# Rotary products of the queries moved from GpSimd to VectorE, with a padded hidden layer and another form of floor

## What is computed

```python
qkv = x @ Wqkv
q, k, v = jnp.split(qkv, 3, -1)
q = l2norm(q) * qs
k = l2norm(k) * ksc
q = q * cos * scale + rotate_half(q) * sin * scale
k = k * cos * inv + rotate_half(k) * sin * inv
out = local_attention(q, k, v)
return out @ Wo
```

## Time and profile before

| | us |
|---|---|
| median of 3 runs | 3893.35 |
| lowest and highest of them | 3887.17, 3898.36 |
| profiled execution, whole | 3903.03 |
| its span, first to last instruction | 3901.3 |
| transformer stage, first to last mask product, about | 1778 |

### The profile page before, as it was taken

How to read it: one execution, slowest core, us unless ns; L and a number is a source line. 1 busy time by engine, 2 the same in 40 slices (tenths; PEclk the granted TensorE clock), 3 DMA queues, 4 the chain that set the end, 5 groups by cost and what they waited for, 6 DMA issues and landing times. The chain is left out here.

```text
span 3901.3 us, 124853 instructions
## 1 busy us (share of the span) xinstructions
PE 3535.7 (91%) x52653; PEld 2416.1 (62%) x52653; DVE 2444.6 (63%) x5150; ACT 2288.7 (59%) x4664; POOL 2084.5 (53%) x2227
## 2 busy tenths in 40 slices
PE   7996999998999988999999999999999996968885
PEld 4664555544566655766676666676676775846664
DVE  4446445512566646777777777677677775568885
ACT  2233555522455555766776676676676775457775
POOL 2003000000121128888888888888888884177773
PEclk9997999999899999999999999999999997989997
DMA  1000000010000003112112211211211111121010
GB/s 27 2 3 24 1 1 1 1 31 7 1 2 2 2 18 85 48 49 70 47 48 60 58 48 46 73 47 45 72 48 46 47 48 25 31 79 24 21 24 20
DMA packets 155562, 130.09 MB, mean 33 GB/s; under 512 B 53592, under 2 KB 144768, under 8 KB 154112
## 3 DMA queue, kind: packets, MB, share of 16 engines
q1 hardware_dynamic: 155008, 122.09, 12.0%
HBM read 31.93 MB, written 3.54 MB: 9 GB/s over the span
## 5 line engine op out<-in xcount | busy, mean ns | idle before, releaser
L1055 PE MATMUL t_wa<-t_w_qkv,t_resid 128*128 128x512 f32 x1152 | 606.6, 627 | 16.2 <-DMA t_scales<-in_L_ffn_k_scale 11.8
L999 POOL TENSOR_TENSOR t_ra<-t_qn,t_rot 128x512 f32<-128x512 f32 x384 | 490.1, 1276 | 179.3 <-DVE t_qn L1310 175.4
L1205 ACT ACTIVATE t_sq<-t_wa 128x512 f32<-128x512 f32 x384 | 227.6, 593 | 172.8 <-PE t_wa L1055 171.7
L3037 DVE TENSOR_REDUCE a_nmax<-a_A 128x2 f32<-128x1024 f32 (+3 forms) x256 | 206.1, 823 | 126.9 <-PE a_A L2935 124.6
L1345 DVE TENSOR_REDUCE t_nmax<-t_S 128x8 f32<-128x512 f32 x192 | 132.8, 692 | 238.1 <-PE t_S L1077 232.7
L1000 POOL TENSOR_TENSOR t_rb<-t_qn,t_rot 128x256 f32<-128x256 f32 x384 | 279.8, 729 | 0.0
L1001 POOL TENSOR_TENSOR t_rb<-t_qn,t_rot 128x256 f32<-128x256 f32 x384 | 279.6, 728 | 0.0
L3030 POOL TENSOR_SCALAR_AFFINE_SELECT a_pt<-a_pt 128x512 f32<-128x512 f32 x128 | 79.7, 634 | 371.9 <-ACT a_pt L3010 371.9
L1299 DVE TENSOR_REDUCE t_ssq<-t_sq 128x8 f32<-128x512 f32 x384 | 261.1, 683 | 17.9 <-ACT t_sq L1205 12.7
L1310 DVE SCALAR_TENSOR_TENSOR t_qn<-t_inv,t_wa 128x512 f32<-128x512 f32 x384 | 249.7, 680 | 13.0 <-POOL t_rb L1001 5.7
L1055 PEld LDWEIGHTS t_wa<-t_w_qkv,t_resid 128*128 128x128 f32 x1152 | 186.7, 195 | 113.9 <-issue 88.2
(11 more groups left out here) (498 smaller groups left out, 9340.0 us busy)
## 6 DMA issues: line engine op xcount, KB each, us to landing
t_vw<-t_vn SPq DMA_DIRECT2D x768, 66.0 KB
t_vw<-t_vn SPq DMA_DIRECT2D x672, 33.0 KB
t_w_qkv<-in_L_ffn_Wqkv SPq DMA_DIRECT2D x6, 1536.0 KB, 6.6
t_v<-t_vn SPq DMA_DIRECT2D x56, 132.0 KB, 2.8
t_vw<-t_nothing SPq DMA_DIRECT2D x96, 33.0 KB
t_w_o<-in_L_ffn_Wo SPq DMA_DIRECT2D x6, 512.0 KB
f_h<-t_L_ffn_h_w SPq DMA_DIRECT2D x2, 1024.0 KB, 7.5
t_w<-in_L_ffn_W SPq DMA_DIRECT2D x6, 341.0 KB
```

The lines of the kernel that those rows point to most:

```text
L999: pool.tensor_tensor(ra[:, n % 2, r], qn[:, r], spread(cos, 1, 8), ALU.mult).then_inc(done.sem, 1)
L1055: pe.matmul(bank, resid[:, b, lo:lo + P], w_qkv[:, l % 2, at:at + 512], start=True, stop=True).then_inc(wa_up.sem, 1)
L1205: act.activation(sq[:, r].rearrange("p h d -> p (h d)"), wa[:, wa_job[kind, n] % 3, :], ACT.Square).then_inc(squared.sem, 1)
L3037: v.tensor_reduce(nmax[:, u % 2, t, :].rearrange("p (j e) -> p j e", e=32)[:, 2 * pair:2 * pair + 2, 0], A[:, 2 * pair:2 * pair + 2, 0:(t ...
```

## The change

- The queries are no longer normalised before the rotation. VectorE multiplies them with cosine and sine straight from the PSUM bank (`rotate_queries`, three instructions for each group, issued between `add_ffn` and the sum of the keys' squares). GpSimd adds the two parts and then, once `inv` is there, scales the sum by it, which commutes with the rotation. The keys keep their path, with `kn` in place of `qn[:, 1]`.
- The bank of the queries is claimed when ScalarE's squares and VectorE's three products of the group before are done.
- The floor is a reduction by maximum over pairs: `ssq` gets a second column that holds 1e-24, the sums are written to the first, and the result goes to `floor_ssq`.
- The third piece of the hidden layer is padded from 85 to 128 columns or rows in `w_1`, `w_2` and `b_1`. GpSimd fills the padding with zeros at the start, and SyncE's first load waits for all seven fills (before, the loads went first and the wait for four fills came behind).
- The banks are named by a table `WA` in place of the job number modulo 3. The order of the projections is left as it is.

```diff
+    WA = {"q": 0, "k": 1, "v": 2}
...
-        w_1 = st.sb("w_1", [P, 2, 2 * hid])
+        w_1 = st.sb("w_1", [P, 2, 2, NH * P])
...
-        ssq = st.sb("ssq", [P, 2, 16])
+        ssq = st.sb("ssq", [P, 2, 16, 2])
+        floor_ssq = st.sb("floor_ssq", [P, 2, 16])
...
-        qn = st.sb("qn", [P, 2, 8, HD])
+        kn = st.sb("kn", [P, 8, HD])
...
-                    sp.dma_start(w_1[:, z, :], w1[l]).then_inc(sem, 16)
+                    sp.dma_start(w_1[:, z, :, 0:hid], w1[l].rearrange("p (h n) -> p h n", h=2)).then_inc(sem, 16)
...
+                sp.wait_ge(zeroed, 7)
                 load(0)
-                sp.wait_ge(zeroed, 4)
...
+                pool.memset(w_1[:, :, :, hid:NH * P], 0.0).then_inc(zeroed, 1)
+                pool.memset(w_2[:, :, NH - 1, :], 0.0).then_inc(zeroed, 1)
+                pool.memset(b_1[:, :, :, NH - 1], 0.0).then_inc(zeroed, 1)
...
-                def rotate(kind, n):
-                    r, done = (0, q_rot) if kind == "q" else (1, k_rot)
+                def rotate_keys(n):
                     t = tile_of(n)
-                    cos, sin = rot[:, layer_of(t) % 2, 2 * r, t % TPB, :], rot[:, layer_of(t) % 2, 2 * r + 1, t % TPB, :]
-                    pool.wait_ge(normed.sem, normed.at(n, r + 1))
+                    cos, sin = rot[:, layer_of(t) % 2, 2, t % TPB, :], rot[:, layer_of(t) % 2, 3, t % TPB, :]
+                    if n % SLOTS == 0:
+                        pool.wait_ge(tables.sem, tables.at(layer_of(t), 6))
+                    pool.wait_ge(normed.sem, normed.at(n))
                     if n >= 2:
-                        pool.wait_ge(T_up.sem, T_up.at(T_job[kind, n - 2]))
-                    pool.tensor_tensor(ra[:, n % 2, r], qn[:, r], spread(cos, 1, 8), ALU.mult).then_inc(done.sem, 1)
-                    pool.tensor_tensor(rb[:, n % 2, r, :, 0:32], qn[:, r, :, 32:64], spread(sin[:, 0:32], 1, 8), ALU.mult).then_inc(done.sem, 1)
-                    pool.tensor_tensor(rb[:, n % 2, r, :, 32:64], qn[:, r, :, 0:32], spread(sin[:, 32:64], 1, 8), ALU.mult).then_inc(done.sem, 1)
+                        pool.wait_ge(T_up.sem, T_up.at(T_job["k", n - 2]))
+                    pool.tensor_tensor(ra[:, n % 2, 1], kn[:, :], spread(cos, 1, 8), ALU.mult).then_inc(k_rot.sem, 1)
+                    pool.tensor_tensor(rb[:, n % 2, 1, :, 0:32], kn[:, :, 32:64], spread(sin[:, 0:32], 1, 8), ALU.mult).then_inc(k_rot.sem, 1)
+                    pool.tensor_tensor(rb[:, n % 2, 1, :, 32:64], kn[:, :, 0:32], spread(sin[:, 32:64], 1, 8), ALU.mult).then_inc(k_rot.sem, 1)
 
                 for even, now, turn, mid, ahead, tail, ffn, last in slots():
                     if ffn is not None:
                         pool.wait_ge(lnd.sem, lnd.at(ffn, 3))
                         pool.tensor_tensor(rstd[:, :], vare[:, :], g["half"][:, 0:1], ALU.pow).then_inc(rooted.sem, 1)
                     if mid is not None:
-                        rotate("k", mid)
+                        rotate_keys(mid)
                         pool.wait_ge(k_rot.sem, k_rot.at(mid, 3))
                         pool.tensor_tensor(ra[:, mid % 2, 1], ra[:, mid % 2, 1], rb[:, mid % 2, 1], ALU.add).then_inc(k_roped.sem, 1)
                     if ahead is not None:
-                        if ahead % SLOTS == 0:
-                            pool.wait_ge(tables.sem, tables.at(layer_of(tile_of(ahead)), 6))
-                        rotate("q", ahead)
                         pool.wait_ge(q_rot.sem, q_rot.at(ahead, 3))
-                        pool.tensor_tensor(ra[:, ahead % 2, 0], ra[:, ahead % 2, 0], rb[:, ahead % 2, 0], ALU.add).then_inc(q_roped.sem, 1)
+                        pool.tensor_tensor(ra[:, ahead % 2, 0], ra[:, ahead % 2, 0], rb[:, ahead % 2, 0], ALU.add).then_inc(q_added.sem, 1)
+                        pool.wait_ge(q_added.sem, q_added.at(ahead))
+                        pool.wait_ge(inved.sem, inved.at(ahead))
+                        pool.tensor_tensor(ra[:, ahead % 2, 0], ra[:, ahead % 2, 0], spread(inv[:, ahead % 2, 0:8], 2, HD), ALU.mult).then_inc(q_roped.sem, 1)
...
+                        elif kind == "k":
+                            pe.wait_ge(normed.sem, normed.at(n - 1))
                         else:
-                            pe.wait_ge(normed.sem, normed.at(n - 1, 1 if kind == "q" else 2))
-                    return wa[:, wa_job[kind, n] % 3, :]
+                            pe.wait_ge(squared.sem, squared.at(n - 1, 1))
+                            pe.wait_ge(q_rot.sem, q_rot.at(n - 1, 3))
+                    return wa[:, WA[kind], :]
...
-                        for c, (at, size) in enumerate(HC):
-                            lo = half * hid + at
-                            m = pe.matmul(bank[0:size, c * P:(c + 1) * P], w_1[:, l % 2, lo:lo + size], lnT[:, :], start=True, stop=True)
+                        for c in range(NH):
+                            m = pe.matmul(bank[:, c * P:(c + 1) * P], w_1[:, l % 2, half, c * P:(c + 1) * P], lnT[:, :], start=True, stop=True)
...
+                v.memset(ssq[:, :, :, 1], 1e-24).then_inc(limits, 1)
+                v.wait_ge(limits, 1)
...
-                    v.tensor_reduce(ssq[:, n % 2, 8 * r:8 * r + 8], sq[:, r], X, ALU.add).then_inc(summed.sem, 1)
+                    v.tensor_reduce(ssq[:, n % 2, 8 * r:8 * r + 8, 0], sq[:, r], X, ALU.add).then_inc(summed.sem, 1)
 
                 def floor(n):
                     v.wait_ge(summed.sem, summed.at(n, 2))
-                    v.tensor_scalar(ssq[:, n % 2, :], ssq[:, n % 2, :], 1e-24, None, ALU.max).then_inc(floored.sem, 1)
-
-                def normalise(kind, n):
-                    r, read = (0, q_rot) if kind == "q" else (1, k_rot)
+                    v.tensor_reduce(floor_ssq[:, n % 2, :], ssq[:, n % 2, :, :], X, ALU.max).then_inc(floored.sem, 1)
+
+                def rotate_queries(n):
+                    t = tile_of(n)
+                    cos, sin = rot[:, layer_of(t) % 2, 0, t % TPB, :], rot[:, layer_of(t) % 2, 1, t % TPB, :]
+                    raw = wa[:, WA["q"], :].rearrange("p (h d) -> p h d", h=8)
+                    v.wait_ge(wa_up.sem, wa_up.at(wa_job["q", n]))
+                    if n % SLOTS == 0:
+                        v.wait_ge(tables.sem, tables.at(layer_of(t), 6))
+                    if n >= 2:
+                        v.wait_ge(T_up.sem, T_up.at(T_job["q", n - 2]))
+                    v.scalar_tensor_tensor(out=ra[:, n % 2, 0], in0=spread(cos, 1, 8), scalar=LIFT ** 0.5, in1=raw, op0=ALU.mult, op1=ALU.mult).then_inc(q_rot.sem, 1)
+                    v.scalar_tensor_tensor(out=rb[:, n % 2, 0, :, 0:32], in0=spread(sin[:, 0:32], 1, 8), scalar=LIFT ** 0.5, in1=raw[:, :, 32:64],
+                                           op0=ALU.mult, op1=ALU.mult).then_inc(q_rot.sem, 1)
+                    v.scalar_tensor_tensor(out=rb[:, n % 2, 0, :, 32:64], in0=spread(sin[:, 32:64], 1, 8), scalar=LIFT ** 0.5, in1=raw[:, :, 0:32],
+                                           op0=ALU.mult, op1=ALU.mult).then_inc(q_rot.sem, 1)
+
+                def normalise_keys(n):
                     v.wait_ge(inved.sem, inved.at(n))
                     if n:
-                        v.wait_ge(read.sem, read.at(n - 1, 3))
-                    v.scalar_tensor_tensor(out=qn[:, r], in0=spread(inv[:, n % 2, 8 * r:8 * r + 8], 2, HD), scalar=LIFT ** 0.5,
-                                           in1=wa[:, wa_job[kind, n] % 3, :].rearrange("p (h d) -> p h d", h=8),
+                        v.wait_ge(k_rot.sem, k_rot.at(n - 1, 3))
+                    v.scalar_tensor_tensor(out=kn[:, :], in0=spread(inv[:, n % 2, 8:16], 2, HD), scalar=LIFT ** 0.5,
+                                           in1=wa[:, WA["k"], :].rearrange("p (h d) -> p h d", h=8),
                                            op0=ALU.mult, op1=ALU.mult).then_inc(normed.sem, 1)
...
                         add_ffn(last)
                     if ahead is not None:
+                        rotate_queries(ahead)
                         sums("k", ahead)
...
-                        normalise("q", ahead)
-                        normalise("k", ahead)
+                        normalise_keys(ahead)
```

27 lines of the change are left out of this document (14 added, 13 removed).

## The result

| | before | after |
|---|---|---|
| median, us | 3890.86 (4 runs) | 3944.94 (4 runs) |
| lowest and highest | 3887.17, 3898.36 | 3943.92, 3945.92 |
| profiled execution | 3903.03 | 3943.92 |
| its span | 3901.3 | 3942.2 |

The ratio is 1.0136, with the interval 1.0119 to 1.0154: the change makes the kernel 54 us slower, 1.4%. The direction came out as forecast, and so did the mechanism of the ordinary slots; the size is half, for the ordinary slots were priced too high and a gain at the weight loads had no term.

What follows compares the result with a forecast made beforehand. TensorE was taken as nearly the bound, with VectorE's work ahead of the weighted output setting its time. Ordinary slots +113, tables -16 and start +7 gave +104 on the median 3893.35, so 3997 us; range 3955 to 4060.

Steps and rivals of the forecast that it cites:

- The block: VectorE's three query products ahead of the keys' sum cost 0.59 + 0.33 + 0.33 = 1.25 us per slot (1.1 to 1.5).
- Nothing hides it in the even slot: Even slot, with head mixing: the products delay the weighted output, and TensorE's `turn_o` starts 0.93 us later.
- The odd slot: Slot without head mixing: waits cover part of the products' time, and the slot's end moves by 0.32 us.
- The floor: VectorE's floor as a reduction takes 0.19 us and waits for nobody, against a median of 0.396 before.
- a floor that still waits: Bound on the forecast: if the reduction still waited, 0.2 to 0.3 us more each, 58 us in all.
- The tables: Five layer-boundary slots: VectorE makes the rotary tables undisturbed by GpSimd, 3.3 us earlier each, -16 us (0 to -27).
- The start: SyncE's first loads wait for all of GpSimd's fills, so TensorE begins later: +7 us, once.
- five times behind other work: Weight loads: `w_1` comes as twice as many runs of half the size, five times, at no cost.
- Faster: Rival: waits for the weighted output (38 us) and the tables' 16 vanish, giving 3846 us; chance 0.05.
- within 0.3%: Rival: products overlap with reductions, odd slot free, even one costs 0.1 us, giving 3894 us; chance 0.04.
- TensorE's clock falls: Rival: gaps of 0.9 us in each even slot lower TensorE's granted clock, giving 4093 us; chance 0.07.
- Dearer terms: Rival, same mechanism: half products at 0.46 us and a floor that waits in places, up to 4060 us; chance 0.16.

Runs made afterwards that it cites:

- floor: The kernel before with the new floor alone, a reduction over pairs in place of the old maximum: 3889.84 us, ratio 0.9987.
- oldfloor: The kernel after with the old floor, a tensor_scalar maximum in place, instead of the reduction: 3997.25 us, ratio 1.0265.
- moved: The kernel after with the queries' three products issued ahead of the residual's update in even slots and last in odd ones: 3853.25 us, ratio 0.9897.
- pad: The kernel before with the hidden layer's padding and the wait for seven fills ahead of the first load: 3902.79 us, ratio 1.0019.
- floorpad: The kernel before with the reduction floor, the padding and the wait for seven fills, without the products' move: 3897.32 us, ratio 1.0005.
- after_load9: The kernel after with each next layer's weights loaded one slot later: 3944.33 us, ratio 1.0124.
- after_late2: The kernel after with each weight load held back within its slot, starting 6.6 us in instead of 1.6 to 2.2: 3962.82 us, ratio 1.0183.
- before_load9: The kernel before with each next layer's weights loaded one slot later: 3873.54 us, ratio 0.9953.

## Why the prediction was right or wrong

**The block, right.** Forecast 1.25 us, measured 1.27. The half product takes 0.414 us with a step of 0.33, as chosen (0.42, 0.33), well inside the bounds of 0.26 to 0.46. By the formula of the Trainium skill ("VectorE: DVE Perf Modes", the section on the TRN2 errata) the half was 0.39; the measurement differs from it by 0.02.

**Nothing hides it in the even slot, right; its price, 0.15 too high.** The mean growth is 0.78 us, not 0.93. The term that failed is the step from the floor to the reciprocal, set at 0.22 us and measured at 0.11, for the reciprocal begins before the reduction ends. That is most of the 0.15. The rest is the example: its sum of the keys started 6.19 us into the slot, where the mean is 6.11, and the block starts at 6.09. The means of `turn_o`'s start are 8.41 before and 9.17 after, a shift of 0.75, and 0.03 more come behind it.

That step does not hang on the form of the floor. In `floor`, with the same reduction, it is 0.22 in 95 even slots:

```profile
2868.84 0.19 DVE L1307 TENSOR_REDUCE t_floor_ssq<-t_ssq 128x16 f32<-128x32 f32 x1
2869.06 0.21 DVE L1374 RECIPROCAL t_rden<-t_S 128x8 f32<-128x8 f32 x1
```

In `oldfloor` the reciprocal starts 0.08 ahead of the old floor's end, as it does behind the reduction in the kernel after. What tells the kernels apart is the instruction with which VectorE last read PSUM. In the eight where that is the second half of the residual's update, at partition 64 (before, `floor`, `moved` and others), the reciprocal starts 0.03 us behind the floor's end; in the six where it is the block, at partition 0 (after, `oldfloor` and others), it starts 0.08 ahead of it. No run varied this alone, so it is a reading and not shown.

**The odd slot, too high as well.** 0.186 instead of the 0.25 that is left of 0.32 once the sum has taken off 0.07 for the example's short wait. `turn_o` starts 0.32 us later (means 6.69 and 7.01 into the slot) and not 0.59. The floor starts 5.60 us into the slot where 5.67 was reckoned, the norm follows its start after 0.10 and not after 0.17, and in the example the reciprocal of before stood at 5.59 where the mean is 5.71. The cover was of the right kind: the copy `oT` moves by 0.18, less than `turn_o`, and the slot's end follows the copy. `moved`, which takes the block out of the odd slot's chain, gives all of the 0.19 back (9.028). Together the ordinary slots and those at the loads cost 94 x 0.781 + 89 x 0.186 = 90 us (96 pairs would be 93); the forecast was 113 for 96 pairs.

**The floor, right, and worth more than its own saving.** Constant at 0.186, forecast 0.19. The term for "a floor that still waits" was 58 us; `oldfloor` shows 50 to 52. It was put evenly on 192 slots, and it lies in the 96 even ones.

**The tables, somewhat more.** -21 us, forecast -16, within the bound of -27. The five slots take 10.3 us, in the range of 10 to 11 given. VectorE makes the tables from 1760.69 to 1762.37 in the boundary slot, 1.68 us for the 4.31 of the earlier trace rows.

**The start.** The first load is issued at 1465.03 instead of 1457.13, 7.9 us later, and TensorE's first projection comes at 1473.84 instead of 1465.92: the term of +7 was right there. The first mask product is only 4.6 us later in this pair of profiles, but 8.5 and 8.4 in `pad` and `floorpad` (1493.98 and 1493.87 for 1485.45); between profiles of kernels that differ in nothing ahead of it (after, `after_load9`, `after_late2`: 1490.04, 1491.63, 1487.36) it moves by some 4 us. Where those come from is open.

**What the sum lacked: the stalls at the loads, -30 us.** This is the step that failed most. The forecast reckoned with ordinary slots and with boundary slots. It put the loads at nothing, as "five times behind other work", and has no row of the slots behind them, where the kernel before loses 3.3 to 4.9 us and some slow products each time, 121.8 - 10 x 9.01 = 31.7 us in all. No row of the waits shows them, since they stand there as "issue". In the kernel after the excess is 96.2 - 5 x (9.751 + 9.228) = 1.3 us. That the stalls come and go with the moment at which the load is issued is shown by `before_load9` and `after_late2`, worth 18 us each by the ratios. That they went with the move of the products, and neither with the floor nor with the padding, is shown by the 17 of 20 loads against 2 of 35. The stall ends with the arrival of a late instruction packet (2.2 to 2.5 us behind its start, 24 of 24), and it goes with the count between two packets (444 or more in 22 cases, all with a stall; 410 or fewer in 48, 46 without). What makes a packet come 4.6 us behind one load and 9.6 behind another was not settled, and with it stays open how the move of the products acts on it, by its content or only by the places at which TensorE's list is cut. The distance of the last packet alone doesn't tell: in `floor` one 5.2 us ahead of the load goes with a gap of 4.0 us, in the kernel after one 4.5 ahead with none. From the forecast of +104 to the 41 us of the profiles it is 63: 30 for the stalls, 23 for the ordinary slots, 5 for the tables, 2 for the start and 2 for the edges. The profiled executions differ by 41 us and the medians by 54; 12 of these 13 us are the profiled execution of before, which lies above its median.

**The rivals.** Faster (3846) did not come about, for the reason given against it; nor did "within 0.3%", for the even slot pays in full. That TensorE's clock falls was wrong: gaps of 0.65 us in each even slot leave the granted clock of the stage at 1.00, higher than the 0.98 of before. There it stood at 0.50 for 3.4 to 6.8 us behind each of the five stalls at the loads (gaps of 3.3 to 4.9 us) and in each of the five boundary slots (gaps of up to 3.4 us), and in the kernel after both kinds of gap are gone. Dearer terms: only in `oldfloor`. GpSimd's later keys appear in no wait of TensorE's that counts, and its 304 us less of work (forecast 276) were worth nothing in the ordinary slots; the gain of 21 us in the table slots is VectorE's, as forecast.

## What to carry to other kernels

What is moved to another engine costs by where it stands in that engine's list: before moving work, look for idle time in the receiving list that lies before the wait on which the chain hangs, here 1.41 us for a block of 1.27, and issue it there. A wait of a short instruction on a shared resource is worth measuring in the kernel with the change and not in the one without: the same floor was worth 5 us in one and some 50 in the other. And read every kind of slot in the trace, also those behind a large transfer; a gap of TensorE in the middle of a run of like products, put down to "issue", is time that a shift of the transfer by one slot can bring back, as it did here by 0.5%.

## What the runs showed of the hardware

- TensorE stood still for 1.9 to 4.9 us at a load of 1.5 MB of weights in all 22 cases in which it had begun 444 or more products and weight loads since the last of its instruction packets (250 is the mean), and started again 2.2 to 2.5 us behind the start of the next one. In the kernel before and in `after_late2` the granted clock stood at 0.50 (1.2 GHz) for 3.4 to 6.8 us behind each of these gaps. Issuing the load 4.5 us later in the kernel after caused the gap at all five loads, issuing it one slot later in the kernel before removed it.
- On VectorE the reciprocal starts 0.08 us ahead of the end of the short instruction before it in the even slots of six kernels (after, `oldfloor` and others) and 0.03 behind that end in those of eight (before, `floor`, `moved` and others), with either form of the floor.
- GpSimd's product of 128x512 elements with `inv` spread over 64 took 1.044 us in all 192 cases, while its addition of the same size takes 1.27.
